# The first graph convolution's projection placed inside the second mixing stage, and weight parts of a convolution split ahead of time

## The reference

```python
# mix, per head: k and v are normalised over the head's 64 elements
qkv = x @ w_qkv.T ; dots = k.T @ v ; out = q @ dots / N ; mix = out @ w_out.T + b_out
# graph layer, twice (k = 0, 1), A = weighted adjacency with self loops, d = deg ** -0.5
xw = temp @ W_k ; conv = d * (A.T @ (d * xw)) + b_k ; temp = 0.9 * conv + 0.1 * temp
# block: x = x + graph(xn) + mix(xn), xn = layernorm(x)
```

## Time and profile before

| | us |
|---|---|
| median of 3 runs | 2266.91 (2265.09 to 2268.65) |
| the profiled execution | 2265.84 |
| its span, first to last instruction | 2264.3 |
| PE busy | 2094.6, 93% |
| DVE busy | 1653.3, 73% |
| ACT busy | 1233.8, 54% |

### The profile page before, as it was taken

The page is one execution under the profiler, slowest core; times in us unless marked ns, Lnnn a source line. Parts: engine busy times, 40 slices in busy tenths (PEclk is TensorE's granted clock), DMA queues, the critical chain, the costliest instruction groups (busy, mean ns, idle before and its releaser), DMA issues. The chain is left out here.

```text
span 2264.3 us, 47270 instructions
## 1 busy us (share of the span) xinstructions
PE 2094.6 (93%) x18287; PEld 1966.4 (87%) x18287; DVE 1653.3 (73%) x3119; ACT 1233.8 (54%) x2875; POOL 569.9 (25%) x406
## 2 busy tenths in 40 slices
PE   5559999999879999998999999999999999999996
PEld 3348999999769999997778999899988999999996
DVE  6888877778388888885657655556657867888885
ACT  5565555555437676675533444444435336677674
POOL 3000000000016777773000000000000014777775
PEclk9789999999989999999999999999999999999998
DMA  3413333333547778776001666366651025777776
GB/s 122 142 59 105 102 89 89 112 95 89 160 157 217 222 225 240 222 225 169 20 25 50 184 194 188 98 196 188 188 156 63 20 92 173 226 225 237 232 220 170
DMA packets 241114, 339.04 MB, mean 150 GB/s; under 512 B 33407, under 2 KB 202546, under 8 KB 240754
## 3 DMA queue, kind: packets, MB, share of 16 engines
q1 hardware_dynamic: 208908, 296.19, 41.6%
q0 software_dynamic: 28528, 35.76, 8.5%
q10 hardware_dynamic: 3446, 3.97, 0.5%
HBM read 258.89 MB, written 76.95 MB: 148 GB/s over the span
## 5 line engine op out<-in xcount | busy, mean ns | idle before, releaser
L1977 POOL DMA_INDIRECT SC<-xd,slot_i x128 | 186.5, 1457 | 1461.3 <-DVE slot_q L1613 1332.4
L2371 PE MATMUL bank<-WB_r,XN_r 128*128 128x448 f32 x1400 | 399.7, 367 | 3.7 <-DVE WB_r L2330 3.7
L2330 DVE TENSOR_TENSOR WB_r<-WB,WB_r 128x448 fp32r<-128x448 f32 x350 | 214.0, 624 | 166.1 <-ACT WB_r L2323 166.1
L2323 ACT CAST WB_r<-WB 128x448 fp32r<-128x448 f32 x350 | 197.6, 568 | 222.2 <-PE bank L2371 219.1
L2371 PEld LDWEIGHTS bank<-WB_r,XN_r 128*128 128x128 f32 x1400 | 263.2, 188 | 26.8 <-DVE wb__r L2296 4.4
L1907 PE MATMUL bank<-SC_r,WB_r 128*128 128x256 f32 (+1 forms) x2064 | 250.7, 280 | 8.2 <-issue 7.4
L1907 PEld LDWEIGHTS bank<-SC_r,WB_r 128*128 128x128 f32 x2064 | 244.0, 188 | 12.7 <-issue 12.7
L1048 ACT CAST WB_r<-bank 128x200 fp32r<-128x200 f32 x391 | 140.5, 359 | 194.7 <-PE bank L1032 193.4
L1922 PE MATMUL bank<-R_r,H_r 128*128 128x256 f32 x1752 | 215.1, 282 | 4.8 <-DVE R_r L1818 4.8
L1922 PEld LDWEIGHTS bank<-R_r,H_r 128*128 128x128 f32 x1752 | 208.9, 189 | 5.1 <-issue 5.1
L1770 ACT ACTIVATE wb_<-bank,WB 128x256 f32<-128x256 f32 (+1 forms) x344 | 133.2, 476 | 80.0 <-PE bank L1907 41.3
(11 more groups left out here) (463 smaller groups left out, 5130.4 us busy)
## 6 DMA issues: line engine op xcount, KB each, us to landing
WB<-adjw SPq DMA_DIRECT2D x350, 224.0 KB, 2.9
WB<-in_f_pack SPq DMA_DIRECT2D x127, 512.0 KB
WB<-in_f_pack SPq DMA_DIRECT2D x62, 640.0 KB
adjw<-X SPq DMA_DIRECT2D x24, 1600.0 KB, 7.5
WB<-in_f_pack SPq DMA_DIRECT2D x65, 516.0 KB
xd<-XN SPq DMA_DIRECT2D x15, 640.0 KB, 5.5
y<-X SPq DMA_DIRECT2D x10, 640.0 KB, 3.3
X<-y SPq DMA_DIRECT2D x6, 640.0 KB, 6.5
```

Source lines behind the costliest of these rows:

```text
L1977: e.indirect_dma_start(yin[i % 2][:, q * D:(q + 1) * D], None, XD, bass.IndirectOffsetOnAxis(ap=slot_i[:, 2 * i + q:2 * i + q + 1], axis=0 ...
L2323: e.copy(split_w(m)[0], RAW[m % PR]).then_inc(S("whigh"), 1)
L2330: e.tensor_tensor(al, RAW[m % PR], ah.bitcast(F32), ALU.subtract).then_inc(S("wlow"), 1)
L2371: mm_ = e.matmul(conv_bank(k, band, c)[:, 0:PW], x[st][:, o], y, start=(st == 0 and i == 0), stop=(st == T - 1 and i == 2))
```

## The change

The first projection's 25 tiles no longer follow the mix. Tiles 0 to 2 are issued on PE in the last three turns of the keys and values loop, tiles 3 and 4 before RJ, tiles 5 to 7 between RJ and MW, tiles 8 to 24 between MW and the outputs of the mix. On DVE the low parts of the tiles stand at matching places. The first projection uses five banks in turn, the second six in place of eight, the outputs of the mix three in place of four. RJ and MW put two results into one bank, so DVE copies twice 128x512 and once 128x512 in place of six times 128x256. `bd`, `rj`, `mw` and the low parts move to other memory. The first convolution waits for DVE's additions of tiles 23, 22 and 24 before the bands whose banks the outputs used. The low parts of the first convolution's first five pieces are taken on DVE between the outputs of the mix (after tiles 3, 7, 11, 15 and 19), and the high and low parts of the second convolution's first five pieces stand ahead of the second projection. No loads are added or removed; the function that issues them is the same.

```diff
-    bd = R1[:, 0, 0:512].rearrange("p (j n) -> p j n", j=4)
-    rj = R1[:, 0, 512:1536].rearrange("p (j n) -> p j n", j=4)
-    mw = R1[:, 1, 0:512].rearrange("p (c n) -> p c n", c=2)
-    MIXP_RJ, MIXP_MW, MIXP_OUT = 0, 4, 6
-    MIXV_BD, MIXV_RJ, MIXV_MW, MIXV_OUT = 0, 1, 5, 7
+    bd = SC[:, 3, :].rearrange("p (j n) -> p j n", j=4)
+    rj = wa[:, 1024:2048].rearrange("p (j n) -> p j n", j=4)
+    mw = SC[:, 2, :].rearrange("p (c n) -> p c n", c=2)
+
+    MIXP_RJ, MIXP_MW, MIXP_OUT = 0, 2, 3
+    MIXV_BD, MIXV_RJ, MIXV_MW, MIXV_OUT = 0, 1, 3, 4
+    RJ_BANKS, MW_BANK = (0, 3), 7
+
+    def out_bank1(t):
+        return B[(7, 3, 0)[t % 3]]
+
+    def project_bank(k, t):
+        return B[t % 6] if k else B[(5, 6, 4, 1, 2)[t % 5]]
...
+        for t in range(3):
+            project_low(e, 0, t)
         e.wait_ge(S("dots"), T)
         e.scalar_tensor_tensor(bd, dt4, 1.0 / N, mask64.unsqueeze(1).to_broadcast([128, 4, 128]),
                                ALU.mult, ALU.mult).then_inc(S("mixed_dve"), 1)
-        for j in range(4):
-            e.wait_ge(S("mixed_pe"), MIXP_RJ + j + 1)
-            e.tensor_copy(rj[:, j, :], B[j][:, 0:D]).then_inc(S("mixed_dve"), 1)
+        for t in range(3, 5):
+            project_low(e, 0, t)
         for i in range(2):
-            e.wait_ge(S("mixed_pe"), MIXP_MW + i + 1)
-            e.tensor_copy(mw[:, i, :], B[4 + i][:, 0:D]).then_inc(S("mixed_dve"), 1)
+            e.wait_ge(S("mixed_pe"), MIXP_RJ + i + 1)
+            e.tensor_copy(rj[:, 2 * i:2 * i + 2, :], B[RJ_BANKS[i]].rearrange("p (j n) -> p j n", j=2)).then_inc(S("mixed_dve"), 1)
+        for t in range(5, 8):
+            project_low(e, 0, t)
+        e.wait_ge(S("mixed_pe"), MIXP_MW + 1)
+        e.tensor_copy(mw, B[MW_BANK].rearrange("p (c n) -> p c n", c=2)).then_inc(S("mixed_dve"), 1)
+        biases_dve(e, c)
+        for t in range(8, T):
+            project_low(e, 0, t)
         for t in range(T):
             e.wait_ge(S("mixed_pe"), MIXP_OUT + t + 1)
-            e.tensor_tensor(X[:, t, :], X[:, t, :], B[t % 4][:, 0:D], ALU.add).then_inc(S("mixed_dve"), 1)
+            e.tensor_tensor(X[:, t, :], X[:, t, :], out_bank1(t)[:, 0:D], ALU.add).then_inc(S("mixed_dve"), 1)
             e.wait_ge(S("mixed_dve"), MIXV_OUT + 2 * (t + 1) - 1)
             e.tensor_tensor(X[:, t, :], X[:, t, :], bout1, ALU.add).then_inc(S("mixed_dve"), 1)
+            if t % 4 == 3 and t // 4 < PR - 1:
+                weight_low(e, t // 4)
...
             if t >= T:
+                project_tile_pe(e, 0, t - T)
                 continue
...
+        for t in range(3, 5):
+            project_tile_pe(e, 0, t)
         e.wait_ge(S("mixed_dve"), MIXV_BD + 1)
...
-            e.matmul(B[j][:, 0:D], bd[:, j, :], wo1[:, j, :], start=True, stop=True).then_inc(S("mixed_pe"), 1)
-        e.wait_ge(S("mixed_dve"), MIXV_RJ + 4)
+            m = e.matmul(B[RJ_BANKS[j // 2]][:, j % 2 * D:(j % 2 + 1) * D], bd[:, j, :], wo1[:, j, :],
+                         start=(j % 2 == 0), stop=(j % 2 == 1), skip_group_check=True)
+            if j % 2:
+                m.then_inc(S("mixed_pe"), 1)
+        for t in range(5, 8):
+            project_tile_pe(e, 0, t)
+        e.wait_ge(S("mixed_dve"), MIXV_RJ + 2)
         for c in range(2):
             for j in range(4):
-                m = e.matmul(B[4 + c][:, 0:D], wq[:, j, c * 128:(c + 1) * 128], rj[:, j, :], start=(j == 0), stop=(j == 3))
-            m.then_inc(S("mixed_pe"), 1)
-        e.wait_ge(S("mixed_dve"), MIXV_MW + 2)
+                m = e.matmul(B[MW_BANK][:, c * D:(c + 1) * D], wq[:, j, c * 128:(c + 1) * 128], rj[:, j, :],
+                             start=(c == 0 and j == 0), stop=(j == 3), skip_group_check=True)
+        m.then_inc(S("mixed_pe"), 1)
+        for t in range(8, T):
+            project_tile_pe(e, 0, t)
+        e.wait_ge(S("mixed_dve"), MIXV_MW + 1)
         for t in range(T):
-            if t >= 4:
-                e.wait_ge(S("mixed_dve"), MIXV_OUT + 2 * (t - 3) - 1)
-            e.matmul(B[t % 4][:, 0:D], XT[:, 0, t * 128:(t + 1) * 128], mw[:, 0, :], start=True, stop=False)
-            e.matmul(B[t % 4][:, 0:D], XT[:, 1, t * 128:(t + 1) * 128], mw[:, 1, :], start=False, stop=True).then_inc(S("mixed_pe"), 1)
+            if t >= 3:
+                e.wait_ge(S("mixed_dve"), MIXV_OUT + 2 * (t - 2) - 1)
+            bk = out_bank1(t)
+            e.matmul(bk[:, 0:D], XT[:, 0, t * 128:(t + 1) * 128], mw[:, 0, :], start=True, stop=False)
+            e.matmul(bk[:, 0:D], XT[:, 1, t * 128:(t + 1) * 128], mw[:, 1, :], start=False, stop=True).then_inc(S("mixed_pe"), 1)
...
-    lows = ([r1r[:, i * D:(i + 1) * D] for i in range(16)] + [war[:, i * D:(i + 1) * D] for i in range(8)] + [wbr[:, :]])
+    lows = ([war[:, i * D:(i + 1) * D] for i in range(4)] + [r1r[:, i * D:(i + 1) * D] for i in range(16)]
+            + [war[:, i * D:(i + 1) * D] for i in range(4, 8)] + [wbr[:, :]])
...
-    def project_pe(e, k):
-        src = conv_source(k)
-        for t in range(T):
-            bk = B[t % 8]
-            if t >= 8:
-                e.wait_ge(S("lows"), T * k + t - 7)
-            elif k:
+    def project_tile_pe(e, k, t):
+        src, bk = conv_source(k), project_bank(k, t)
+        if k:
+            if t >= 6:
+                e.wait_ge(S("lows"), T * k + t - 5)
+            else:
                 e.wait_ge(S("cfree"), 2 * last_in(t // 2) + 2)
-            elif t < 4:
-                e.wait_ge(S("mixed_dve"), MIXV_OUT + 2 * (T) - 1)
-            if k:
-                e.wait_ge(S("conv"), convolved_to((t + 1) * 128))
-            for c in range(2):
-                m = e.matmul(bk[:, 0:D], src[:, c, t * 128:(t + 1) * 128], gc[k][:, c, :], start=(c == 0), stop=(c == 1))
-            m.then_inc(S("proj"), 1)
+            e.wait_ge(S("conv"), convolved_to((t + 1) * 128))
+        elif t >= 5:
+            e.wait_ge(S("lows"), t - 4)
+        elif t < 3:
+            e.wait_ge(S("vals"), T - 2 + t)
+        for c in range(2):
+            m = e.matmul(bk[:, 0:D], src[:, c, t * 128:(t + 1) * 128], gc[k][:, c, :], start=(c == 0), stop=(c == 1))
+        m.then_inc(S("proj"), 1)
 
     def project_act(e, k):
         e.wait_ge(S("dinv"), 1)
         for t in range(T):
             e.wait_ge(S("proj"), T * k + t + 1)
-            e.activation(highs[t], B[t % 8][:, 0:D], ACT.Copy, scale=dcol[:, t:t + 1]).then_inc(S("highs"), 1)
-
-    def project_dve(e, k):
-        e.wait_ge(S("dinv"), 1)
-        for t in range(T):
-            e.wait_ge(S("highs"), T * k + t + 1)
-            e.scalar_tensor_tensor(lows[t], B[t % 8][:, 0:D], dcol[:, t:t + 1], highs[t].bitcast(F32),
-                                   ALU.mult, ALU.subtract).then_inc(S("lows"), 1)
+            e.activation(highs[t], project_bank(k, t)[:, 0:D], ACT.Copy, scale=dcol[:, t:t + 1]).then_inc(S("highs"), 1)
+
+    def project_low(e, k, t):
+        if t == 0:
+            e.wait_ge(S("dinv"), 1)
+        e.wait_ge(S("highs"), T * k + t + 1)
+        e.scalar_tensor_tensor(lows[t], project_bank(k, t)[:, 0:D], dcol[:, t:t + 1], highs[t].bitcast(F32),
+                               ALU.mult, ALU.subtract).then_inc(S("lows"), 1)
...
+    def weight_high(e, m):
+        e.wait_ge(S(f"ab{m % PR}"), weights_landed(m))
+        if m >= PR:
+            e.wait_ge(S("wmm"), m - PR + 1)
+        e.copy(split_w(m)[0], RAW[m % PR]).then_inc(S("whigh"), 1)
+
+    def weight_low(e, m):
+        e.wait_ge(S("whigh"), m + 1)
+        ah, al = split_w(m)
+        e.tensor_tensor(al, RAW[m % PR], ah.bitcast(F32), ALU.subtract).then_inc(S("wlow"), 1)
+
     def conv_act(e, k):
-        for n in range(NW):
-            m = NW * k + n
-            e.wait_ge(S(f"ab{m % PR}"), weights_landed(m))
-            if m >= PR:
-                e.wait_ge(S("wmm"), m - PR + 1)
-            e.copy(split_w(m)[0], RAW[m % PR]).then_inc(S("whigh"), 1)
+        for m in range(NW * k + (PR - 1 if k else 0), min(NW * (k + 1) + PR - 1, 2 * NW)):
+            weight_high(e, m)
 
     def conv_dve(e, k, c):
-        def low(n):
...
-        for n in range(PR - 1):
-            low(n)
         for n in range(NW):
             band, st = divmod(n, T)
-            if n + PR - 1 < NW:
-                low(n + PR - 1)
+            if NW * k + n + PR - 1 < 2 * NW:
+                weight_low(e, NW * k + n + PR - 1)
             if st < T - 1:
...
                 e.wait_ge(S("cfree"), 2 * (PB * k + band - 3))
+            if k == 0 and band in (0, 1, 3):
+                e.wait_ge(S("mixed_dve"), MIXV_OUT + 2 * (T - (2, 3, None, 1)[band] + 1) - 1)
...
         mix1_dve(e, c)
-        biases_dve(e, c)
-        project_dve(e, 0)
         conv_dve(e, 0, c)
-        project_dve(e, 1)
+        for t in range(T):
+            project_low(e, 1, t)
...
-        project_pe(e, 0)
         conv_pe(e, 0)
-        project_pe(e, 1)
+        for t in range(T):
+            project_tile_pe(e, 1, t)
         conv_pe(e, 1)
```

(21 more changed lines are left out.)

## The result

The changed kernel takes 2250.93 us, median of 6 runs (2248.20 to 2253.18), against 2266.54 (6 runs) before: ratio 0.9934, interval 0.9921 to 0.9947, so by the ratio 15.0 us less (12.0 to 17.9). The forecast was 9.8 us less, a median of 2257.1 and a range that ended at 2253.5; the measured median lies outside, on the fast side. The profiled execution took 2253.12 us, span 2251.6.

A forecast was written before the change was run, and what follows sets the result against it. PE was taken to bound the kernel. An earlier first convolution (6.1 us), no pause before the second (2.0) and no clock fall there (1.7) made 9.8 us, a forecast median of 2257.1 us, range 2253.5 to 2262.5.

The forecast's parts named there:

- Bound and mechanism: Both convolutions: PE is the bound, so whatever lets PE start a convolution sooner is kept to its end.
- The projection inside the mix: From the dots of tile 23: projection tiles fill PE's pauses, outputs of the mix begin at 1203.1.
- The waits for `rj` and `mw`: PE around RJ and MW: projection tiles cover both waits, cost nothing; without cover each costs its old 0.52 us.
- the wait for `bd`: PE before RJ: `bd`, queued on DVE behind low parts of tiles 0 to 2, leaves 0.5 us open.
- The outputs are now set by DVE: Outputs of the mix: DVE needs 0.863 us a tile plus 2.7 us for five weight parts; first convolution at 1227.5.
- Gain of the first part: Up to the first convolution's start: 1233.59 less 1227.5, 6.1 us, if the clock stays at 2.4 GHz.
- The second part: Second projection to second convolution: weights taken ahead remove the pause, 2.0 us, and the clock fall behind it, 1.7 us.
- The clock in the chain: Dots of tile 23 to first convolution: the old trace's half clock until 1182.4 lost 3.4 us; full clock assumed after.
- the rival about the clock: Around 1175 in the changed kernel: the clock falls all the same, costs 3.4 us, giving 2260.5; chance 0.25.
- The range: Whole kernel: 2253.5 to 2262.5 us, with about 2 us of other clock luck on either side.
- S: Theory of the experiments: a steady 4 us come from outside the dots of tile 23 to the second convolution's end.
- The slower rival: Outputs of the mix: PE waiting for DVE lowers the clock to 1.2 GHz, costing 19 us, giving 2276; chance 0.03.

The follow-up runs named there:

- `e_parts_behind`: Changed kernel with the first convolution's five first low parts on DVE behind all outputs of the mix instead of between them; 2259.13 us, one run.
- c_after2: Changed kernel without edit, run again as a control; ratio 0.9951 (0.9937 to 0.9965) to the kernel before.
- c_before: Kernel before without edit, run again as a control; ratio 0.9992 (0.9980 to 1.0005) to the kernel before.
- c_before2: Kernel before without edit, one look for another trace; 61.44 us from the dots of tile 23 to the first convolution.
- e_second_only: Kernel before with only the second convolution's first five weight pieces ahead of its projection and six banks; ratio 0.9977 (0.9965 to 0.9988).

## Why the prediction was wrong, and where it was right

- **Bound and mechanism: right.** PE's time to each convolution's start is kept to the end. The first convolution takes 214.2 us in both traces.
- **The projection inside the mix: right to 0.2 us.** Predicted start of the outputs 28.2 us after the dots of tile 23 (1203.1 - 1174.94), measured 28.4. DVE was to begin them at 29.6 and began at 29.5. The waits for `rj` and `mw` cost nothing; the wait for `bd` left no pause. The match is in part luck: the 0.5 us left open for `bd` wasn't used, and the terms for dots, tiles and RJ were together 0.7 too short.
- **"The outputs are now set by DVE", at 0.863 us a tile: the failed step in the sum.** Those rows showed DVE without a recorded idle, but at PE's pace, and I took the pace for DVE's own. The next tile's addition follows 0.41 after the bias addition there, and 0.34 when it is truly queued. Predicted 23.0 us from DVE's first addition to the first convolution, measured 21.5. The addition of tile 23 began 1223.03 - 1201.98 = 21.05 after the first, where 23 x 0.863 + 2.7 = 22.55 had been put. This is 1.5 us, and `e_parts_behind` shows the same from the other side. Gain of the first part in the same pair of traces: 7.6, not 6.1.
- **The second part: right in this pair, half of it by luck.** 2.2 us for the pause (2.0 predicted), 1.3 for the clock (1.7), 3.5 in place of 3.7. The pause is there in every trace with the old seam; the fall behind it came in three of five.
- **The clock in the chain: taken from one trace, the second step that failed.** The sum used that trace's fall as if the kernel always had it, and the rival about the clock looked only at falls in the changed kernel. Four traces of the old order average 59.8 us, 1.1 over the one I read; behind the pauses of 1.84 us the clock fell in 4 of 10 cases (1.3 to 1.6 each), where the changed kernel has no such pause. With these the region gives 8.7 + 2.2 + about 1 = **12 us** on average. The sum so mended would have forecast about 2255 (2266.9 - 12), still inside the stated range: these two steps explain some 2 us of the miss, and not that the median came out below 2253.5. The changed kernel's remaining pause of 1.57 us brought no fall in any trace that has it, so the first rival didn't come true.
- **The range: too near on the gain side.** Its text speaks of 2 us of luck on either side, all from the clock; its lower end lies 3.6 under the forecast, and where the other 1.6 come from isn't said. The three measured differences, by the ratios, are 15.0, 13.4 and 11.1 us; 12 lies in the interval of the last two and at the edge of the first (12.0). The first pair also had an early stage that was 8 us shorter in the trace of after. What made that stage short is open, and so is whether it was short in the other five runs. The kernel before took 2266.5 us in the first measurement and 2272 to 2275 in the later sets, so the conditions weren't the same. That luck explains the first measurement's surplus of 3 us is an inference from the controls, not shown. S is not supported by the traces, and 15.6 lies outside the interval of c_after2 (7.9 to 14.3): neither the start of the chain nor what follows the second convolution differs between the kernels.
- **The slower rival** (outputs at 1.2 GHz) did not come: the clock was 1.00 in that stage in every trace. Its condition hardly arose either: it had PE wait for DVE in 11% of the stage, but PE was busy 22.12 of 22.40 us. The Trainium skill's case for this rival, in "TensorE: Matmul & The Clock Gate" under "A second HAM failure mode: psum-queue depth-cycling", small idle times between groups of matmuls, was therefore barely put to the test: two pauses of 0.14 us (the first between the outputs at 1216.85 and 1217.42, 0.57 apart in place of 0.43), and the clock stayed at 2.4 GHz.

## What to carry to other kernels

When two engines move in step, "no idle before it" doesn't tell whose pace it is: look for a place where the engine has a backlog before its pace is put into a sum. Where a serial chain leaves the tensor engine pausing, put independent matmuls of a later stage into the pauses; besides the pauses it takes away the luck of the clock, which one trace of before can't price, so look at several traces of the same kernel. And ask what the engine can do in the first pause: three tiles there in place of one were worth 1.9 us more of the chain.

## What the runs showed of the hardware

- In the four traces of the old order the same 2.44 us pause went with a fall of the clock to 1.2 GHz: for 3.4 us (c_before, beginning only 2.8 us after the pause's end), 6.8 (before) and 13.7 (c_before2, e_second_only). After a pause of 1.84 us it fell in 4 of 10 cases, after 1.57 and 1.60 us in none of 7.
- With ten more matmuls in one pause of 2.44 us the kernel took 6.1 us (3.4 to 8.9) of 2274 less.
- Additions of 128x256 on DVE start 0.45 us apart when the second waits for the first, 0.34 when it doesn't and is queued.
